# Output projection of twelve token tiles in pairs, by Strassen's seven block products in place of eight

## What is computed

```
xn = _layernorm(x, axis=-1)
s = _L0_attn_ref(xn, L0_attn_Wq, L0_attn_Wk, L0_attn_Wv, L0_attn_Wo)   # ... out @ Wo at its end
g = _silu(_L0_ffn_ref(xn, L0_ffn_weight, ...))
x = x + s * g
```

## Time and profile before

| quantity | value |
|---|---|
| time, median of 3 runs | 1168.62 us (1168.09 to 1170.62) |
| the profiled execution: its own time | 1168.28 us |
| its span, first to last instruction | 1166.5 us |
| PE busy in the span | 1134.9 us (97%) |
| DVE, ACT, POOL busy | 723.2, 611.2, 421.8 us |
| granted TensorE clock, mean over the span | 0.994 of full speed |
| the third stage, from tile 1 on | 997.3 us to the end |

### The profile page before, as it was taken

How to read it: one execution, slowest core, us unless ns; L and a number is a source line. 1 busy time by engine, 2 the same in 40 slices (tenths; PEclk the granted TensorE clock), 3 DMA queues, 4 the chain that set the end, 5 groups by cost and what they waited for, 6 DMA issues and landing times.

```text
span 1166.5 us, 17720 instructions
## 1 busy us (share of the span) xinstructions
PE 1134.9 (97%) x5692; PEld 946.1 (81%) x5692; DVE 723.2 (62%) x1731; ACT 611.2 (52%) x1286; POOL 421.8 (36%) x254
## 2 busy tenths in 40 slices
PE   5899999999999999999999999999999999999998
PEld 3677767788888888888888888888888887888886
DVE  6756542477767777677776777767767678324222
ACT  6545543266655666556665566655666577412211
POOL 0434537343343433424334243342523434222120
PEclk9899999999999999999999999999999999999999
DMA  9425132210202202022360220202202034564753
GB/s 373 187 90 235 50 96 102 80 56 18 63 9 72 61 11 63 9 72 63 144 216 9 72 63 9 63 9 72 63 9 63 9 106 174 171 206 153 216 187 119
DMA packets 87271, 112.01 MB, mean 96 GB/s; under 512 B 3408, under 2 KB 68944, under 8 KB 86224
## 3 DMA queue, kind: packets, MB, share of 16 engines
q1 hardware_dynamic: 87248, 111.72, 28.9%
HBM read 78.15 MB, written 33.55 MB: 96 GB/s over the span
## 4 chain that ended last, share of the span: by engine, by line
PE 88%; DVE 5%; ACT 3%; POOL 1%; issue 1%; DMA 1%; SPq 0%; DVEq 0%; ACTq 0%; POOLq 0%
PE at_proj L44 17%; PE at_proj L46 17%; PE at_proj L45 17%; PE at_out L975 7%; PE ff_z_ps L287 6%; PE at_pt L962 6%; PE at_score L944 3%; PE at_score L945 3%; PE at_score L46 2%; PE at_score L45 2%; PE at_score L44 2%; POOL ff_xs_lo L676 1%; PE at_proj L929 1%; DVE xs_full L598 1%; ACT ff_xs_hi L419 1%
## 5 line engine op out<-in xcount | busy, mean ns | idle before, releaser
L44 PE MATMUL at_proj<-xn_hi,w_hi 128*128 128x512 f32 x896 | 361.9, 404 | 1.6 <-POOL w_lo L1400 0.8
L46 PE MATMUL at_proj<-xn_hi,w_lo 128*128 128x512 f32 x896 | 351.2, 392 | 0.0
L45 PE MATMUL at_proj<-xn_lo,w_hi 128*128 128x512 f32 x896 | 349.6, 390 | 0.0
L46 PEld LDWEIGHTS at_proj<-xn_hi,w_lo 128*128 128x128 f32 x896 | 168.3, 188 | 37.0
L44 PEld LDWEIGHTS at_proj<-xn_hi,w_hi 128*128 128x128 f32 x896 | 168.7, 188 | 31.8 <-issue 1.2
L45 PEld LDWEIGHTS at_proj<-xn_lo,w_hi 128*128 128x128 f32 x896 | 169.0, 189 | 30.3
L1384 POOL TENSOR_TENSOR at_turning<-at_turning,rope_table 128x512 f32<-128x512 f32 x64 | 82.9, 1296 | 289.3 <-DVE at_turning L1228 289.3
L1392 POOL TENSOR_TENSOR w_lo<-w_stage,w_hi 128x1024 fp32r<-128x1024 f32 x45 | 114.5, 2559 | 162.8 <-ACT w_hi L1060 162.8
L1098 ACT ACTIVATE at_prob<-at_score,at_neg_max 128x512 f32<-128x512 f32 (+3 forms) x256 | 133.3, 526 | 71.2 <-DVE at_neg_max L1256 70.8
L1107 ACT ACTIVATE at_pt_hi<-at_pt 128x512 fp32r<-128x512 f32 (+1 forms) x192 | 93.9, 524 | 99.9 <-PE at_pt L962 99.2
L1273 DVE TENSOR_TENSOR at_pt_lo<-at_pt,at_pt_hi 128x512 fp32r<-128x512 f32 (+1 forms) x192 | 112.0, 597 | 42.2 <-ACT at_pt_hi L1107 41.2
(11 more groups left out here) (125 smaller groups left out, 1824.4 us busy)
## 6 DMA issues: line engine op xcount, KB each, us to landing
z_store<-z SPq DMA_DIRECT2D x16, 512.0 KB, 2.9
w_stage<-in_L_attn_Wq_dram SPq DMA_DIRECT2D x16, 512.0 KB, 3.8
w_stage<-in_L_attn_Wk_dram SPq DMA_DIRECT2D x16, 512.0 KB, 5.1
w_stage<-in_L_attn_Wv_dram SPq DMA_DIRECT2D x16, 512.0 KB, 6.2
att_store<-at_att_t SPq DMA_DIRECT2D x32, 256.0 KB, 2.0
rope_table<-att_store SPq DMA_DIRECT2D x16, 512.0 KB, 6.6
z<-_attn_hidden_states_dram SPq DMA_DIRECT2D x16, 512.0 KB, 4.8
at_turning<-z_store SPq DMA_DIRECT2D x16, 512.0 KB, 6.1
```

Of the source, the lines that this page charges most:

```text
L44: pe.matmul(out, sh, mh, start=first, stop=False)
L45: pe.matmul(out, sh, ml, start=False, stop=False)
L46: return pe.matmul(out, sl, mh, start=False, stop=final)
```

## The change

Tiles 0 to 3 stay as they are in PE's work. Tiles 4 to 15 are taken in six pairs, called rounds q = 0 to 5 here, with n = 4 + 2q for the first tile of a pair. The two tiles' attention rows and the two halves of the inner dimension are a 2 x 2 block matrix A. Wo is a 2 x 2 block matrix B by halves of both dimensions. Winograd's form of Strassen's scheme gives the four output blocks by seven block products, each 4 inner blocks by 3 matmuls = 12 matmuls of 128x512, where the plain way has eight.

The seven products use sums of blocks:

- Of the weights, four sums T1 to T4. They are made once, during tiles 0 to 3. SP loads the rows of Wo again in four steps of two 512 KB transfers (`load_rows`). For each step DVE makes four sums of 128x512 (`sums`), ACT their high parts (`sums_high`), DVE and POOL two low parts each (`sums_low`).
- Of the attention tiles, four sums S1 to S4 for each round, on DVE (`row_sums`). ACT makes the high parts of the seven operands (`op_hi`), each 128x512, DVE the low parts of the four sums (`op_low`), POOL those of A11, A12 and A22.

PE's products in a round are P1 = A11, P2 = A12, P3 = S2, P4 = S1, P5 = S3, P6 = S4, P7 = A22, on three PSUM banks a, b and c. Several products add onto what a bank holds. Since a partial result is used twice, ACT copies it out in between (`part_copy`, three for each round). P3 waits for the copy of bank a after P1, P5 for the copy of bank a after P3, P6 for the copy of bank c after P4. P7 waits until DVE has read bank a after P5. Then `block_out` and `block_21` on DVE form the four output blocks: add the copied part (three of the four), multiply by silu, add x.

The result is formed in the tile of x itself. So `load_x(n)` waits for `y_out`, which says that the store of tile n - 2 has landed.

The core of the diff (the buffers of the attention loop are released, and their space holds the sums):

```diff
-            def load_xz(n):
+            def load_z(n):
                 if n >= 2:
                     sp.wait_ge(y_add, n - 1)
+                sp.dma_start(z_tile[:, n % 2, :], z_store[tile_rows(n), :]).then_inc(xz_in[n % 2], 16)
+
+            def load_x(n):
+                if n >= 2:
+                    sp.wait_ge(y_out[n % 2], 16 * (n // 2))
                 sp.dma_start(x_tile[:, n % 2, :], io["x"][tile_rows(n), :]).then_inc(xz_in[n % 2], 16)
+
+            def store_y(n):
+                sp.wait_ge(y_add, n + 1)
+                sp.dma_start(out[tile_rows(n), :], x_tile[:, n % 2, :]).then_inc(y_out[n % 2], 16)
...
+            load_att(2)
+            load_rows(2)
+            store_y(0)
+            load_z(2)
+            load_att(3)
+            load_x(2)
+            store_y(1)
+            load_z(3)
+            load_x(3)
+            load_rows(3)
+            load_att(4)
+            load_att(5)
+            store_y(2)
+            load_z(4)
+            load_x(4)
+            store_y(3)
+            load_z(5)
+            for n in range(PLAIN, TILES, 2):
+                more = n + 2 < TILES
+                if more:
                     load_att(n + 2)
...
+                    load_att(n + 3)
+                load_x(n + 1)
+                store_y(n)
+                if more:
+                    load_z(n + 2)
+                    load_x(n + 2)
+                store_y(n + 1)
+                if more:
+                    load_z(n + 3)
...
+            def strassen(q):
+                a, b, c = banks[q % 2]
...
+                pe.wait_ge(op_low_pool, 3 * q + 1)
+                product(a, A11, wo_block(0, 0), True)
+                pe.wait_ge(op_low_pool, 3 * q + 2)
+                product(b, A12, wo_block(1, 0), True)
...
+                pe.wait_ge(partial_ok, 3 * q + 1)
+                product(a, S2, wo_sum_block(T2), False)
...
+                product(c, S1, wo_sum_block(T1), True)
...
+                pe.wait_ge(partial_ok, 3 * q + 2)
+                product(a, S3, wo_sum_block(T3), False)
...
+                pe.wait_ge(partial_ok, 3 * q + 3)
+                product(c, S4, wo_block(1, 1), False)
...
+                pe.wait_ge(block_read, 3 * q + 2)
+                product(a, A22, wo_sum_block(T4), False)
...
+            def part_copy(q, which):
+
+                act.wait_ge(product_done, 7 * q + (1, 3, 4)[which])
+                if q >= 1:
+                    act.wait_ge(block_done, 3 * (q - 1) + (1, 3, 2)[which])
+                act.activation(partial[:, which, :], banks[q % 2][(0, 0, 2)[which]][:], ACT.Copy).then_inc(partial_ok, 1)
...
+            for q in range(ROUNDS_W):
+                n = PLAIN + 2 * q
+                more = q + 1 < ROUNDS_W
+                part_copy(q, 0)
+                silu(n, 0)
+                silu(n + 1, 1)
+                part_copy(q, 1)
+                if more:
+                    op_hi(q + 1, A11)
+                    op_hi(q + 1, A12)
+                    op_hi(q + 1, S2)
+                part_copy(q, 2)
+                if more:
+                    for op in (S1, S3, S4, A22):
+                        op_hi(q + 1, op)
...
+            def block_out(q, which, p, o, last):
...
+                dve.wait_ge(product_done, 7 * q + (2, 6, 5)[which])
...
+                dve.tensor_tensor(part, banks[q % 2][(1, 2, 0)[which]][:], part, ALU.add).then_inc(block_read, 1)
...
+                dve.wait_ge(silu_done, n + 1)
+                dve.tensor_tensor(z, part, z, ALU.mult).then_inc(block_done, 1)
...
+                ins = dve.tensor_tensor(x, x, z, ALU.add)
+                if last:
+                    ins.then_inc(y_add, 1)
...
+            for q in range(ROUNDS_W):
+                more = q + 1 < ROUNDS_W
+                block_out(q, 0, 0, 0, False)
+                if more:
+                    row_sums(q + 1)
+                    op_low(q + 1, S2)
+                    op_low(q + 1, S1)
+                block_out(q, 2, 1, 1, False)
+                if more:
+                    op_low(q + 1, S3)
+                block_out(q, 1, 0, 1, True)
+                if more:
+                    op_low(q + 1, S4)
+                block_21(q)
```

271 lines of the change are left out of this document (222 added, 49 removed).

## The result

The changed kernel takes 1209.69 us (median of 4, 1208.9 to 1212.57), the kernel before 1169.23 us beside it. The ratio is 1.0349, with a 95% interval of 1.0335 to 1.0363: 40.5 us slower. The forecast was 1204 us. The profiled execution took 1208.9 us, with a span of 1207.1.

The account below looks back on a forecast made before the run. PE set the pace before; in the changed rounds a chain of transfers, silu and copy would. Span 1166.5 + 9.5 before round 0 + 27.0 in rounds - 1.1 tail = 1201.9, plus 1.8 and 0.3: 1204 us, range 1181 to 1226.

Parts of the forecast that it names:

- P1 of round 0: Weight sums beside tiles 0 to 3 delay the first round from 1030.05 to 1039.5: +9.5 us, 7 without DVE-POOL exclusion.
- P1 to P5 in round 0: First store some 9 us after the round's start, five transfers 9.8, the rest 1.8; P5 at 20.3 us.
- P5 to the first store: ACT's and DVE's operations 8.3 us, plus 0.7 for DVE-POOL hindrance, plus the lower clock's unhidden part: 9.9 us.
- what the change takes off PE: In the rounds, 84 matmuls where a pair had 96: 19.04 us instead of 21.76, 16.3 us over six rounds.
- the lighter rival: Same chain, but DVE and POOL don't meet and the clock stays: 1189 us, chance 0.2 for 1180 to 1192.
- the 0.7 us for DVE and POOL before the first store: Between P5 and the first store, POOL's two low parts hinder DVE: 0.7 us added, half of one low part.
- of which DVE's own lateness hides 1.5: P5's 12 matmuls at the lower clock take 2.4 us more; DVE being late anyway hides 1.5 of it.
- with no such exclusion the sum would be about 6 us less: If DVE and POOL did not exclude each other on SBUF, the sum would be about 6 us less.
- The forecast's price for all of the clock: PE's clock falls after idling before P5 in each round; without the clock's part the sum is 5 us less.
- Heavier: Clock also falls in tiles 2 and 3 and through P6, transfers 1.7 to 1.8 us: 1218 to 1235 us, chance 0.1.
- Fast transfers: In the rounds, 512 KB transfers take 1.23 us, a round 22.2 us: 1173 to 1184 us, chance 0.05.
- PE stays the bound: In the rounds, x arrives early enough to hide copy and silu, so the change pays: down to 1151 us, chance 0.06.

Follow-up runs that it names:

- experiment 1: Changed kernel with ScalarE's second copy, the high parts of A11, A12, S2, S1 and the third copy ahead of the second tile's silu: 1189.1 us.
- 5: Changed kernel with separate semaphores for x and z, and one attention load ahead of the pair's stores, the other right behind them: 1186.8 us.
- 6: As 5, with four slots of x from tile 6 on, so that each x is issued a round ahead: 1179.0 us.
- 9: As 6, with ScalarE's order of experiment 1 on top: 1166.4 us, ratio to the kernel before 0.9958 to 0.9982.
- 4: Changed kernel with two of three matmuls in each block product, the low part of the attention operand left out: 1199.7 us.
- Experiment 7: Changed kernel with the low parts of A11, A12 and A22 made by DVE instead of POOL: 1210.9 us.
- Experiment 3: Changed kernel with 22 extra matmuls into an unused PSUM bank ahead of P5's waits, to keep PE busy: 1202.4 us.
- 10: Changed kernel with another order in tiles 0 to 3 (gates ahead of the weight sums' low parts, attention loads and stores earlier), all work kept: 1208.1 us.
- experiment 12: As kernel 11, with the high and low parts of the first pair's A11 and A12 ahead of the last weight sums' parts: 1163.4 us.
- experiment 8: Changed kernel with only the first k's weight sums loaded and made, and read for all four k: 1200.9 us.
- kernel 11: 9 and 10 together, all edits that shortened the kernel: 1163.2 us, ratio to the kernel before 0.9933 to 0.9960.

## Why the prediction was right, and where it was off

| step | forecast | measured |
|---|---|---|
| tile 3 starts | 1024 | 1025.17 |
| last rows of Wo land | near 1030 | 1031.2 |
| P1 of round 0 | 1039.5 | 1040.71 |
| P1 to P5 in round 0 | 20.3 | 20.1 |
| P5 to the first store | 9.9 | 9.5, 10.2, 10.7, 10.3, 10.5 |
| first store to the silu of the second tile | 14.6 | 14.6, 14.5, 15.6, 15.1 |
| silu to P5 | 1.8 | 1.7 |
| P5 to P5, rounds 0 to 4 | 26.3 | 26.8 |
| last round: first store to P5 | 11.4 + 1.8 | 14.0 |
| tail | -1.1 | -1.15 |
| whole, on the span | +35.4 | +40.6 |

**The mechanism held.** Every step of the chain stands in the profile where the prediction put it, and experiments 1, 5, 6 and 9 take it apart: TensorE's own work does not set the round (4), the silu ahead of the copy (1, 9), the shared semaphores with the order of the loads (5) and the slot that x shares with the result (6) do. With all of them gone the rounds take 19.3 us, near the 19.04 of "what the change takes off PE". How much the slot costs by itself was measured only on top of 5. The missing 5.2 us are small shares: 1.2 in front of round 0; 4 x 0.5 in the four full rounds; 0.6 between the fifth P5 and its store and 0.8 between that store and the last P5; 0.9 behind the last P5; less 0.2 in round 0, all rounded. Two of them are the clock's. The forecast left it out in front of round 0, but behind the wait of 3.04 us ahead of tile 3 matmuls start 0.43 us apart from 1026.71 to 1030.08, 1.6 us more. Behind the last P5 it took about as much again (1194.00 to 1197.35, below).

Two numbers of the forecast do not follow from its own terms. Round 0: 9 + 9.8 + 1.8 is 20.6 and not 20.3; measured were 8.0 + 10.4 + 1.7, so two small errors cancel, and the close match of that row (20.1) is partly luck. And the lighter rival gives round 0 24.9 us, where 20.3 + 8.2 is 28.5: that rival would have come out near 1193, not 1189.

**One step was wrong in its reason: the 0.7 us for DVE and POOL before the first store**, together with "of which DVE's own lateness hides 1.5". At the lower clock P5 ends 5.3 to 5.5 us after its start, and DVE, which has lengthened low parts ahead of `block_out`, still waits 1.3 to 1.5 us for it. So as long as the clock is low the meetings cost nothing on this path, and the forecast's remark that "with no such exclusion the sum would be about 6 us less" does not hold for the rounds. By the forecast's own terms it could not: without the 0.7, DVE's lateness would hide 0.8 of the 2.4 and not 1.5, and the first store would still come at 9.9. Experiment 7, which took all meetings out of the rounds and put three operations on DVE in their place, gained nothing. Experiment 3 restored the clock and gained 1.5 to 1.9 us a round, where the forecast had 0.9. There DVE was late by 0.9 us, behind a low part lengthened by a meeting, and not by the 1.5 of the forecast. The sum of the terms was right (9.9 for 9.5 to 10.7), the split was not: the meetings have 0 and the clock 1.5 to 1.9 while DVE waits for P5, and with the clock restored a meeting lies inside the 8.7 us. A kernel with the clock restored and the meetings gone was not run. The forecast's price for all of the clock was 5 us; experiment 3 gained 7.3. The rule of the Trainium skill ("SBUF — State Buffer", "SBUF: two separate sides") agrees with the records, 1.82 us for an addition beside POOL's 1.29, but what it costs depends on whether DVE has slack, and in the rounds of the changed kernel it had.

**Where the meetings can cost** is the other place that the prediction named, tiles 0 to 3. There the edits that moved a wait found it again behind a DVE that works nearly all the time (10, 12), and less work was what helped (8). The forecast had +9.5 there, and +7 without them; it was +10.7. How much of it the meetings are was not measured alone; by the estimate in 10 they are about a third of DVE's busy time there, and 8 removes work and meetings together.

**Against the rivals.** "The same chain, lighter" needed the clock to stay, and it fell behind every wait before P5 (2.6 to 7.6 us). "Heavier" had one thing right, the fall in front of round 0, but P6 ran almost whole at the full pace. "Fast transfers" fell: in the burst window 269 GB/s over 13 us are 3.5 MB, 6.7 transfers of 0.524 MB, so 0.85 x 13 / 6.7 = 1.65 us each (taken: 1.63). "PE stays the bound" needed x to pass the queued loads. That is what experiments 6 and 9 built, and with 10 on top (11) the change pays: 1163.2 against 1169.3 us, while six rounds should give 6 x (21.76 - 19.34) = 14.5 us. The rounds of kernel 11 gave 12.9, and about 9 of it go to the weight sums (P1 at 1039.0 for 1030.05).

## What to carry to other kernels

Less arithmetic on the engine that sets the pace was paid for here in the order of everything else: when the result is formed in an input's buffer, the next load waits for the store to land, and each transfer queued behind it inherits that wait. Look for the one in-order engine where such a wait stands ahead of something that the bound engine needs (here a silu ahead of a copy), give each wait its own semaphore and each prefetched input its own slot, and expect the second limit to appear at once when the first is gone. Count the one-time work, too: here it cost about 9 of the 14.5 us that the rounds could win.

## What the runs showed of the hardware

The clock does not answer a gap at once. In the last round of the changed kernel PE was idle for 2.64 us before P5 (PE's timeline):

```profile
1192.48 0.47 PE L44 MATMUL at_proj<-at_wo_sum_hi,w_hi 128*128 128x512 f32 x1 [2.64 <-ACT at_partial L1387]
...
1193.71 0.49 PE L46 MATMUL at_proj<-at_wo_sum_hi,w_lo 128*128 128x512 f32 x1
1194.00 0.63 PE L44 MATMUL at_proj<-at_wo_sum_hi,w_hi 128*128 128x512 f32 x1
...
1197.35 0.40 PE L46 MATMUL at_score<-xn_hi,w_lo 128*128 128x512 f32 x1
```

The first six matmuls kept the 2.4 GHz pace, and only those from 1194.00 to 1197.35 ran at 1.2 GHz, in the middle of dense work. In experiment 1 a gap of 2.86 us was followed by the lower pace from its first matmul on (0.56 us from 1087.71 to the next). Idle times of nearly one length had both outcomes. A third outcome is none at all: behind the 2.38 us ahead of tile 2 in the changed kernel the pace stayed full, and behind 2.18 us at the same place in experiment 8 it fell after six matmuls. So when the level changes was not settled here. And moving POOL's work moves its cost on DVE: in experiment 12 two POOL operations moved 8 us forward lengthened two of DVE's by 1.1 and 1.0 us, and two others, which they had lengthened before, became shorter by as much.
